# Single fp32 down products in the second layer's experts of a two-layer kernel

## What is computed

```
logits = x @ router_w + router_b
probs = jax.nn.softmax(logits, axis=-1)
top_v, top_i = jax.lax.top_k(probs, TOP_K)
gates = jnp.sum(jax.nn.one_hot(top_i, E + 1, dtype=x.dtype) * top_v[..., None], axis=-2)
h = jax.nn.gelu(jnp.einsum('btd,edf->ebtf', x, w1), approximate=False)
y = jnp.einsum('ebtf,efd->ebtd', h, w2)
out = jnp.einsum('bte,ebtd->btd', gates[..., :E], y) + gates[..., E:] * x
```

## Time and profile before

| | |
|---|---|
| median of 3 runs | 2161.85 us (2158.87 to 2163.43) |
| profiled execution | 2164.05 us, span 2162.2 us |
| mean granted TensorE clock | 0.918 |
| second layer's experts | 1643 to 2162 us of the span |
| busy: PE, DVE, ACT, POOL | 1803.6, 1595.5, 956.8, 773.5 us |

### The profile page before, as it was taken

One profiled execution on the slowest core, in us unless ns is written; L12 is line 12 of the kernel. 1 busy time (PEld: TensorE's weight loads), 2 busy tenths in 40 slices (PEclk: granted clock), 3 DMA queues, 4 the chain that ended last, 5 costly groups with the idle time before them and its releaser, 6 DMA issues. The chain is left out here.

```text
span 2162.2 us, 26501 instructions
## 1 busy us (share of the span) xinstructions
PE 1803.6 (83%) x7924; PEld 1132.4 (52%) x7924; DVE 1595.5 (74%) x2752; ACT 956.8 (44%) x1789; POOL 773.5 (36%) x707
## 2 busy tenths in 40 slices
PE   2777777765399999989999899998997776889998
PEld 1344444434266665646556465564554554556666
DVE  5555555526766697886977969779699799878887
ACT  1355555543233423324334243342434754676666
POOL 2233233320000094772846718457184165100000
PEclk9988888885599999999999999999998998999999
DMA  7333333301023335323333233332330000000000
GB/s 260 92 90 91 90 97 103 93 23 65 20 107 112 99 107 170 98 79 93 88 88 97 78 92 87 88 96 84 88 89 15 1 5 5 6 1 6 5 5 10
DMA packets 100396, 157.88 MB, mean 73 GB/s; under 512 B 10005, under 2 KB 48622, under 8 KB 97097
## 3 DMA queue, kind: packets, MB, share of 16 engines
q1 hardware_dynamic: 98855, 155.47, 24.2%
q10 hardware_dynamic: 1442, 1.26, 0.2%
HBM read 123.27 MB, written 33.42 MB: 72 GB/s over the span
## 5 line engine op out<-in xcount | busy, mean ns | idle before, releaser
L1572 ACT ACTIVATE e_gu<-psum 128x512 f32<-128x512 f32 (+1 forms) x368 | 219.1, 597 | 667.4 <-PE psum L1317 526.4
L1315 PE MATMUL psum<-e_hhi,e_ring 128*128 128x512 f32 x704 | 480.4, 682 | 40.3 <-DVE e_hm L1775 32.2
L1324 PE MATMUL psum<-e_hm,w_d 128*128 128x512 f32 (+1 forms) x736 | 383.3, 603 | 14.8 <-DVE e_x L1704 12.2
L1771 DVE TENSOR_TENSOR e_gu<-psum,e_gu 128x512 f32<-128x512 f32 x352 | 241.2, 685 | 184.6 <-PE psum L1354 169.4
L1850 POOL TENSOR_TENSOR e_prod<-e_state,e_phi 128x512 f32<-128x512 f32 x256 | 360.2, 1445 | 16.7 <-DVE e_state L1727 7.3
L295 DVE TENSOR_REDUCE at_negm<-psum 128x2 f32<-128x512 f32 x256 | 165.2, 685 | 175.3 <-PE psum L171 173.7
L1316 PE MATMUL psum<-e_hhi,e_ring 128*128 128x512 f32 x704 | 282.8, 402 | 0.0
L1317 PE MATMUL psum<-e_hlo,e_ring 128*128 128x512 f32 x704 | 281.7, 400 | 0.0
L1775 DVE TENSOR_TENSOR e_hm<-psum,e_gu 128x512 f32<-128x512 f32 x352 | 243.4, 691 | 12.1
L1811 DVE TENSOR_TENSOR e_hm<-psum,e_gu 128x512 f32<-128x512 f32 x256 | 176.6, 690 | 72.3 <-ACT e_gu L1603 36.9
L1315 PEld LDWEIGHTS psum<-e_hhi,e_ring 128*128 128x128 f32 x704 | 137.7, 196 | 147.3 <-issue 75.6
(11 more groups left out here) (244 smaller groups left out, 3039.5 us busy)
## 6 DMA issues: line engine op xcount, KB each, us to landing
e_ring<-w_split SPq DMA_DIRECT2D x308, 256.0 KB, 2.6
qk_parts<-at_part SPq DMA_DIRECT2D x96, 192.0 KB, 2.7
w_split<-e_ring SPq DMA_DIRECT2D x44, 256.0 KB, 2.0
at_qs<-qk_parts SPq DMA_DIRECT2D x16, 576.0 KB
at_ks<-qk_parts SPq DMA_DIRECT2D x16, 576.0 KB
w_gu<-in_w SPq DMA_DIRECT2D x2, 2048.0 KB, 10.1
sel_buf_r<-w_split SPq DMA_DIRECT2D x14, 256.0 KB, 2.7
w_gu<-in_wg SPq DMA_DIRECT2D x1, 2904.0 KB
```

What stands on the lines that cost most here:

```text
L1315: pe.matmul(out, w_hi, x_hi, start=first, stop=False)
L1324: mm = pe.matmul(ps[:, ACC, :], weights_at(T, WD + P * j, P)[0:rows(j), :], hm[0:rows(j), slot(j), :], start=(j == 0), stop=(j == HT - 1))
L1572: a(act_g[0:r, j % 2, :], ps[0:r, GB[j % 2], :], ACT.Silu).then_inc(silu_done, 1)
L1771: ins = v.tensor_tensor(product, ps[0:r, UB[j % 2], :], act_g[0:r, j % 2, :], ALU.mult)
```

## The change

The row `hm` gets four slots and is used raw, in fp32. The copies `hidden_high` and `hidden_low` go, and the halves of w2 with them. The down product is one fp32 matmul, which waits for `m_done` (the `hm` product), in place of three fp32r matmuls that waited for the low half. Each down product now increments `down1_done`; VectorE waits for it before it writes a slot of `hm` again (four tiles back) and before it adds the result. The first down product waits once for the weights' DMA.

```diff
@@ tensor
+                if k == 0 and j == 0:
+                    pe.wait_ge(T["ffn1_loaded"], 32)
+                pe.wait_ge(m_done, T1 * c + j + 1)
+                pe.matmul(ps[:, ACC, :], weights_at(T, w2_low(j), P), hm[:, j % RING1, :], start=(j == 0), stop=(j == T1 - 1))\
+                    .then_inc(down1_done, 1)
-                if k == 0:
-                    pe.wait_ge(w2l_done, j + 1)
-                pe.wait_ge(ml_done, T1 * c + j + 1)
-                s = j % RING1
-                mm = three(ps[:, ACC, :], part(w2_high(j)), part(w2_low(j)), m_hi[:, s, :], m_lo[:, s, :], j == 0, j == T1 - 1)
-                if j == T1 - 1:
-                    mm.then_inc(acc1_done, 1)
@@ scalar
-            def hidden_high(c, j):
-
-
-                act.wait_ge(m_done, T1 * c + j + 1)
-                a(m_hi[:, j % RING1, :], hm[:, j % 2, :], ACT.Copy).then_inc(mh_done, 1)
-
...
-                        if j == W2_FIRST:
-                            act.wait_ge(acc_done, CHUNKS)
-                        for i in w2_tiles(j):
-                            a(part(w2_high(i)), weights_at(T, w2_low(i), P), ACT.Copy).then_inc(w2h_done, 1)
-                    if j > 0:
-                        hidden_high(c, j - 1)
-                    elif k > 0:
-                        hidden_high(c - 1, T1 - 1)
@@ vector
-            def hidden_low(c, j):
-                dve.wait_ge(mh_done, T1 * c + j + 1)
-                v.tensor_tensor(m_lo[:, j % RING1, :], hm[:, j % 2, :], m_hi[:, j % RING1, :].bitcast(F32), ALU.subtract).then_inc(ml_done, 1)
-
             def result(m):
-                dve.wait_ge(acc1_done, m + 1)
+                dve.wait_ge(down1_done, T1 * (m + 1))
...
-                    if k > 0 or j >= 2:
-
-                        dve.wait_ge(ml_done, g - 1)
-                    v.tensor_tensor(hm[:, j % 2, :], ps[:, RB[e % 2], :], gu[:, j % 2, :], ALU.mult).then_inc(m_done, 1)
+                    if k > 0 or j >= RING1:
+
+                        dve.wait_ge(down1_done, g - RING1 + 1)
+                    v.tensor_tensor(hm[:, j % RING1, :], ps[:, RB[e % 2], :], gu[:, j % 2, :], ALU.mult).then_inc(m_done, 1)
                     if k == 0:
                         if j + AHEAD < T1:
                             low_of(w1_low, w1_high, w1h_done, w1l_done, j + AHEAD)
-                        for i in w2_tiles(j):
-                            low_of(w2_low, w2_high, w2h_done, w2l_done, i)
-                    if j > 0:
-                        hidden_low(c, j - 1)
-                    elif k > 0:
-                        hidden_low(c - 1, T1 - 1)
```

More of the change, by code:

```diff
@@ L1078, in w2_low @@
     return WU + P * j
-def w2_high(j):
-    return WD + P * j
 def w1_high(j):
@@ L1130, in experts @@
         w_slots = [ring[:, s * CHUNK:(s + 1) * CHUNK] for s in range(4)] + [T["sel_buf_r"][:, SEL:SEL + CHUNK]]
-        m_lo = ring[:].rearrange("p (s c) -> p s c", c=CHUNK)
-        m_hi = T["sel_buf_r"][:].rearrange("p (s c) -> p s c", c=CHUNK)
         null = weights_at(T, NULL_AT, CHUNK)
@@ L1201, in experts @@
         split_in = [sem(f"split_in{s}") for s in range(W_SLOTS)]
-        w1h_done, w1l_done, w2h_done, w2l_done = (sem(n) for n in ("w1h_done", "w1l_done", "w2h_done", "w2l_done"))
+        w1h_done, w1l_done = sem("w1h_done"), sem("w1l_done")
         up1_done = sem("up1_done")
@@ L1208, in experts @@
         m_done = sem("m_done")
-        mh_done, ml_done = sem("mh_done"), sem("ml_done")
-        acc1_done = sem("acc1_done")
+        down1_done = sem("down1_done")
         acc1_read = sem("acc1_read")
@@ L1261, in run @@
                 block1(q, PEELED1)
[L1263 to L1268, removed]
         def rows(j):
@@ L1621, in _ @@
             run(act, block0, block1)
-            hidden_high(CHUNKS - 1, T1 - 1)
         @block.vector
@@ L1831, in _ @@
             run(dve, block0, block1)
-            hidden_low(CHUNKS - 1, T1 - 1)
             result(CHUNKS - 1)
```

## The result

The changed kernel takes 2125.60 us (2124.72 to 2129.49), the kernel before 2161.85 in the same comparison: a ratio of 0.9835 with an interval of 0.9812 to 0.9857, 36 us faster.

The account below looks back on a forecast made before the run. TensorE paces steady chunks, VectorE the peeled ones: peeled 303 to 271 (-32), steady and last +15.9, together -16 from 2161.85: 2146 us. Range 2129 to 2162.

Parts of the forecast that it names:

- the price of the fp32 matmul: Each tile on TensorE: 0.866 us replaces 0.696, +5.4 us a chunk; rival 2 had 0.93 us, whole kernel 2162, chance 0.10.
- peeled: the rest of TensorE's work: Peeled chunks: old busy time plus 5.4 each, less restarts and low clock, gave 61.3, 59.3, 57.4 and 60.3 us.
- peeled: waits: Peeled chunks: start-up, table loads, hand-overs, edges, router's burst and state additions; 33 us with low clock, called the unknown.
- peeled: low clock: First and second peeled chunk: 3.5 us each at 1.2 GHz; rival 3, low clock stays: +3, 2165 us, chance 0.12.
- last chunk: Last chunk, 58.77 us before: 30 down products +5.1, less 0.6 at the accumulator and 0.3 at the end: +4.2.
- Start-up: First peeled chunk: TensorE waits 4.5 us, from the 5.1 weight-half wait halved and 2 for the late first row.
- Table loads: First, second and fourth peeled chunks: pairs of ScalarE table loads exceed its slack by some 1.2 us, 2.4 a chunk.
- the slack: Time an engine may be late before TensorE stops: 3.1 us for VectorE's hm, 1.6 us for ScalarE's gelu.
- The router's burst: Second peeled chunk: some 7 us on VectorE less the slack of 3.1, a TensorE wait of 4 us.
- Hand-overs: Peeled chunks: the projection's hand-overs cost 2.2 us in the first, hand-overs 1 us in the fourth.
- Edges of the peeled chunks: Each of the four peeled chunks: TensorE waits 1.4 us at the chunk's edge.
- The pace of GpSimd: Rival 1, peeled chunks: GpSimd's scan becomes the pace, gain only -6, whole kernel 2156 us; chance 0.12.

Follow-up runs that it names:

- The kernel with the unused halves: Changed kernel, but ScalarE and VectorE still make both halves of every gelu row, which nobody reads: 2166.39 us, ratio 1.0018 to the kernel before.
- The kernel with halves in the steady chunks: Changed kernel with three fp32r matmuls and halves from the fifth chunk on, w2's halves made in the fourth and fifth: 2112.95 us.
- the subtraction alone: Changed kernel, but VectorE still makes one subtraction a tile that nobody reads; ScalarE's copy stays gone: 2163.95 us, one execution.
- ScalarE's copy alone: Changed kernel, but ScalarE still makes the rounded copy of every gelu row, which nobody reads; VectorE's subtraction stays gone: 2138.49 us, one execution.

## Why the prediction missed

Its reading of the regimes held: TensorE paces the steady chunks and pays for the fp32 product, VectorE paced the peeled ones and gives back more than that. So did the price of the fp32 matmul, read from a row of the same operation. What was too small is the gain in the peeled chunks, by 15 of 18 us. By its terms:

| term | forecast | after | difference |
|---|---|---|---|
| peeled: a steady chunk without its waits, four times | 220.0 | 218.4 | -1.6 |
| peeled: the rest of TensorE's work | 18.3 | 10.7 | -7.6 |
| peeled: waits | 25.5 | 19.0 | -6.5 |
| peeled: low clock | 7.0 | 7.3 | +0.3 |
| three steady chunks | +11.7 | +10.3 | -1.4 |
| last chunk | +4.2 | +2.2 | -2.0 |
| start of the block | 0 | +0.9 | +0.9 |

The first row is 4 x (55.83 - 0.68 - 0.55), against 4 x (56.3 - 1.3); the rest of the forecast's TensorE work is 61.3 + 59.3 + 57.4 + 60.3 less 220.0. The low clock is 0.05 x 71.51 + 0.03 x 65.34 + 0.03 x 59.05; the 10.7 is what 255.4 leaves. The first two rows are one error of 9.2 us, that of TensorE's work (229.1 us, where 238.3 was forecast).

**The step that failed most: TensorE's busy time of before as the base.** The prediction took 239.24 us, added the new product, and took off 4.5 for restarts and 18 for the low clock. The work left in after, busy time less low clock, is 58.9, 56.6, 55.2 and 58.4 us, 2.4, 2.7, 2.2 and 1.9 below the forecast. The last of these has no low clock in either kernel, so the low clock's deduction can't be all of it; busy time in a stretch full of waits was longer than the work in it, and more so than the 1 us or so that was allowed. In the fourth chunk one can read it directly: before it exceeds a steady chunk's by 55.94 - 49.56 = 6.4 us, after by 58.43 - 54.60 = 3.8, with the same side jobs. The other way to the same term stood in the trace: the side jobs' own groups hold 14.2 us of records in the kernel before (13.3 after), with which the peeled work would have been forecast at 220 + 14.2, 4 us lower.

The kernel with the unused halves shows the effect by itself, as its TensorE has the same matmuls as the changed kernel's. In its peeled chunks TensorE is busy 248.8 us against 236.4, 12.3 more. Its low clock is 0.04 x 75.93 + 0.11 x 83.62 + 0.07 x 68.31 = 17.0 us against 7.3, so of the 12.3 at most 9.7 are the clock's and at least 2.6 the waits'; in the fourth chunk, at the full clock in both, it is 59.26 against 58.43. The kernel before had 26.6 us of low clock by its windows, of which the prediction took off 18, as TensorE was partly idle. So up to 7.3 us of the 9.2 can be this deduction, all but the fourth chunk's 1.9. How the excess divides between restarts and the clock no run separates.

**Waits.** Named one by one, with TensorE's wait records:
- Start-up: 4.5 forecast, 1.9 + 2.3 = 4.2 found.
- Table loads: 7.2 forecast, 0.6 + 0.8 + 0.8 = 2.2 found, and in the fourth chunk its two pairs together leave no wait of 0.3 us or more. This is the slack's failure: ScalarE may be away for 3.1 us, not 1.6, and a pair with its activation is 1.28 + 0.30 + 1.28 = 2.9 us. Where only that stood between two gelus there was no wait or one of 0.27; the three waits had more in them: ScalarE copied weight halves too (0.60), emptied the projection's banks before the pair (0.76), or waited 0.58 us for VectorE between the loads (0.84).
- The router's burst: 4 forecast, 2.9 found, by VectorE's 3.9 in place of 3.1. In the third chunk 1 was forecast behind the state additions; the one wait of `hm` there, 1.3, comes behind a product of GpSimd, not behind an addition. The sum agrees by luck.
- Hand-overs: 3.2 forecast, 0.8 + 0.2 found.
- Edges of the peeled chunks: 5.6 forecast, 6.1 + 0.9 = 7.0 found. Two of them wait 2.6 us for `h_lo`, where VectorE has more in front of it than in a steady chunk. An error to the other side; the steady edges came to 0.68 + 0.55 where 0.45 + 0.85 was forecast.

**The low clock** held in its sum, 7 forecast and 7.3 found, but in part by luck: the 3.5 behind the router's burst did not come, and 2.0 and 1.8 us came behind the two edge waits of 2.6 us instead, at the start of the second and of the third chunk.

**The last chunk** was forecast against a chunk that had been slowed: its clock was 0.95 in the earlier trace rows, and TensorE's first 8 us of it in the kernel before read so:

```profile
2103.43:2111.43 8.00, 7.00 (x21) 4.76 (x22) 4.54 (x8) 4.47 (x8) 0.00 (x0) 0.79 0.00 0
```

and in after:

```profile
2066.78:2074.78 8.00, 7.45 (x24) 4.20 (x25) 4.16 (x7) 2.51 (x5) 0.00 (x0) 1.00 0.00 1
```

0.21 x 8 = 1.7 us of the 2.0: the chunk of before paid for a low clock behind its edge wait, and the changed one doesn't. The kernel with halves in the steady chunks, whose last chunk has the matmuls of before, reads 0.79 in that chunk's first 8 us again, and the same 58.77.

**The rivals.** The pace of GpSimd did not come, but for one place: VectorE waited 3.0 us for its products in all, which stopped TensorE once, for 1.3 us, and GpSimd no longer waits for a state addition. The fp32 matmul costs 0.86 here, not 0.93. A page's rule was weighed there: the Trainium skill (FP8 and Floating Point Precision, TensorE Precision Notes) has four passes for a true fp32 matmul; 0.86 / 4 = 0.215 us for each agrees with four passes a little shorter than an fp32r matmul's 0.232. The low clock went with its causes: low for 15 us where it was 53.

**The range** took the waits as the only unknown. It put none on the base that they were added to, and that is where the larger part of the miss lies (9.2 of 15.4 us in the peeled chunks).

## What to carry to other kernels

When a pacing engine is relieved, build the new pace from the new bound's operations (here a steady chunk's time plus the side matmuls' own records) and not from its busy time in the stretch that waited: that came out some 2 us a chunk too high here, after the deductions made. VectorE could be away for the slack behind its product plus its own idle time of a tile, and ScalarE for somewhat more than that; both terms scale with the pace, so a change that shortens the tile gives part of its gain back as waits. And where a program has regimes with different bounds, give each the form that suits its bound: the dearer product with less work beside it where VectorE is full, the cheaper one where TensorE is.

## What the chip showed beyond that

VectorE's subtraction lengthened GpSimd's operations. The scan's products have the same shape and count in every version. Before, in the changed kernel, and in the versions with the subtraction alone and with ScalarE's copy alone:

```profile
L1850 POOL TENSOR_TENSOR e_prod<-e_state,e_phi 128x512 f32<-128x512 f32 x39 | 59.9, 1569 | 14.6 <-DVE e_state L1727 7.3 <-DVE e_y L1644 7.1 <-POOL e_phi L1850 0.2
```

```profile
L1808 POOL TENSOR_TENSOR e_prod<-e_state,e_phi 128x512 f32<-128x512 f32 x39 | 56.1, 1473 | 3.4 <-DVE e_y L1613 3.1 <-POOL e_phi L1808 0.2
```

```profile
L1817 POOL TENSOR_TENSOR e_prod<-e_state,e_phi 128x512 f32<-128x512 f32 x39 | 59.8, 1565 | 14.1 <-DVE e_state L1698 7.3 <-DVE e_y L1615 6.6 <-POOL e_phi L1817 0.2
```

```profile
L1820 POOL TENSOR_TENSOR e_prod<-e_state,e_phi 128x512 f32<-128x512 f32 x39 | 56.1, 1476 | 3.4 <-DVE e_y L1625 3.1 <-POOL e_phi L1820 0.2
```

1569 and 1565 ns with the subtraction, 1473 and 1476 without it: some 0.1 us each. ScalarE's copy does nothing to them. The Trainium skill (SBUF - State Buffer, Terms) says that VectorE and GpSimd share a port pair that one of them holds for a whole instruction; the four lines agree in direction, and show how little it was worth here: 39 x 0.1 = 4 us of GpSimd's time, nearly all of it off the path.
